# One scratch for q and k, and a ring of packed rows by batch instead of by unit

## What is computed

```python
q = proj(w_q, b_q)          # (16, 16 heads, 256, 8)
k = proj(w_k, b_k)
v = proj(w_v, b_v)
scores = jnp.einsum('bhtd,bhsd->bhts', q, k) / jnp.sqrt(jnp.float32(dk))
attn = jax.nn.softmax(scores, axis=-1)
out = jnp.einsum('bhts,bhsd->bhtd', attn, v)
...
x = x + layernorm(attention(layernorm(x)))
x = x + layernorm(experts(layernorm(x)))
```

## Time and profile before

| | |
|---|---|
| median of 3 runs | 526.82 us (524.11 to 530.07) |
| span of the profiled execution | 525.4 us |
| PE busy | 472.5 us (90%) |
| DVE busy | 404.0 us (77%) |
| ACT busy | 372.3 us (71%) |
| POOL busy | 228.4 us (43%) |
| DMA moved | 67.48 MB, 128 GB/s over the span |

### The profile page before, as it was taken

How to read it: one execution, slowest core, us unless ns; L and a number is a source line. 1 busy time by engine, 2 the same in 40 slices (tenths; PEclk the granted TensorE clock), 3 DMA queues, 4 the chain that set the end, 5 groups by cost and what they waited for, 6 DMA issues and landing times.

```text
span 525.4 us, 11035 instructions
## 1 busy us (share of the span) xinstructions
PE 472.5 (90%) x3416; PEld 276.7 (53%) x3416; DVE 404.0 (77%) x1063; ACT 372.3 (71%) x739; POOL 228.4 (43%) x544
## 2 busy tenths in 40 slices
PE   2458998998999999888899899999999999999994
PEld 1212454544544455444346576666666666666662
DVE  4688898989999999768926859788687959687453
ACT  2315887878989988767684576886868696867551
POOL 6054333325444635221003453938567483716241
PEclk9999999999999999989899999999999999999998
DMA  6443334444444433330023353535444644535431
GB/s 197 134 137 109 118 111 133 127 135 132 122 143 142 134 115 105 119 116 29 3 88 120 118 168 97 189 109 178 141 145 161 179 168 122 194 105 192 133 128 40
DMA packets 51737, 67.48 MB, mean 128 GB/s; under 512 B 4192, under 2 KB 35168, under 8 KB 51680
## 3 DMA queue, kind: packets, MB, share of 16 engines
q1 hardware_dynamic: 51680, 66.78, 41.1%
HBM read 51.17 MB, written 15.20 MB: 126 GB/s over the span
## 4 chain that ended last, share of the span: by engine, by line
PE 59%; SPq 12%; DVE 9%; issue 8%; ACT 5%; DMA 5%; POOL 1%; POOLq 0%; DVEq 0%; ACTq 0%
PE pY L1385 8%; PE pS L1385 8%; SPq L408 6%; PE pS L1369 6%; PE pS L1370 6%; PE pS L1371 6%; PE pO L1304 5%; PE pS L1248 5%; SPq L396 4%; DVE mneg L923 4%; DMA k_scratch<-k_parts 2%; DMA qp<-mT 2%; ACT probs L703 2%; PE pS L1254 2%; SPq L416 2%
## 5 line engine op out<-in xcount | busy, mean ns | idle before, releaser
L923 DVE TENSOR_REDUCE mneg<-pS 128x2 f32<-128x512 f32 x256 | 163.7, 684 | 25.0 <-PE pS L1248 24.5
L703 ACT ACTIVATE probs<-pS 128x512 f32<-128x512 f32 x256 | 144.0, 595 | 29.8 <-PE pS L1254 28.2
L1248 PE MATMUL pS<-kp,qp 48*128 48x256 bf16 x512 | 87.4, 290 | 24.4 <-DVE mneg L923 9.3
L789 ACT ACTIVATE h_ring<-r 128x512 f32<-128x512 f32 x104 | 65.0, 625 | 35.0 <-DVE r L1092 26.2
L1369 PE MATMUL pS<-qp,up_hi 128*128 128x512 f32 x144 | 89.3, 620 | 0.0
L1254 PE MATMUL pS<-qp,kp 51*128 51x256 bf16 x512 | 87.1, 281 | 0.9 <-ACT probs L703 0.7
L1304 PE MATMUL pO<-probs,vv 128*32 128x256 f32 x1024 | 74.5, 398 | 0.4 <-ACT oT_sb L655 0.4
L1248 PEld LDWEIGHTS pS<-kp,qp 48*128 48x128 bf16 x512 | 34.2, 96 | 74.8 <-DVE mneg L923 42.4
L1092 DVE SCALAR_TENSOR_TENSOR r<-pS,probs 128x512 f32<-128x512 f32 x64 | 43.4, 686 | 22.2 <-PE pS L1371 21.7
L1092 DVE SCALAR_TENSOR_TENSOR r<-pS,c_ring 128x512 f32<-128x512 f32 x64 | 44.0, 687 | 17.8 <-PE pS L1371 15.4
L1370 PE MATMUL pS<-kp,up_hi 128*128 128x512 f32 x144 | 57.1, 396 | 0.0
(11 more groups left out here) (193 smaller groups left out, 855.5 us busy)
## 6 DMA issues: line engine op xcount, KB each, us to landing
c_ring<-c_scratch SPq DMA_DIRECT2D x32, 512.0 KB, 4.0
probs<-c_scratch SPq DMA_DIRECT2D x32, 512.0 KB, 4.2
qp<-q_scratch SPq DMA_DIRECT2D x64, 96.0 KB
kp<-k_scratch SPq DMA_DIRECT2D x64, 96.0 KB
q_scratch<-q_parts SPq DMA_DIRECT2D x16, 192.0 KB, 2.4
k_scratch<-k_parts SPq DMA_DIRECT2D x16, 192.0 KB, 2.6
q_scratch<-q_parts SPq DMA_DIRECT2D x16, 128.0 KB, 2.6
k_scratch<-k_parts SPq DMA_DIRECT2D x16, 128.0 KB, 2.3
```

The lines of the kernel that those rows point to most:

```text
L703: nc.scalar.activation(probs[j][:, hh], pS2[n % S2_RING][:, :, :], ACT.Exp, scale=SCALE).then_inc(exp_done, 1)
L789: nc.scalar.activation(h_ring[:, (n - at) % HRING], r_sb[n % URING][:, :], ACT.Square).then_inc(sq_done, 1)
L923: nc.vector.tensor_reduce(mneg[u % 2][:, :, hh, k], pS1[n % S1_RING][:, :].rearrange("p (a s) -> p a s", a=TH), AX.X, ALU.max, negate=True ...
L1248: return mm(pS1[n % S1_RING][:, T * th:T * (th + 1)], qp[slot][rows, k, P * th:P * (th + 1)], kp[slot][rows, k, :], start=True, stop=True)
```

## The change

`q_scratch` and `k_scratch` become one `qk_scratch`, in which q and k of the same feature and position lie side by side. The host permutes the rows of the projection weights so that the features come in the order (half of the block pair, feature, unit, block): the eight blocks of a batch are contiguous for one head half and feature. So the row of one slot and feature holds both units, all four blocks of each, q and k: 8 x 2 x 256 bf16 = 8 KB. `load_batch(b)` fetches 48 such rows per half `hh`, two transfers of 384 KB for a batch, where `load_unit` had four of 96 KB for a unit. The ring has three slots of a batch (BRING = 3) with the same memory as six of a unit. The scratch writes keep their number and sizes; their rows of 512 B go to every second 512 B.

`load_batch(b)` waits for the batch's scratch writes, and from batch 3 on for all key scores of the batch that had the slot. In SP's loop `load_batch(b+2)` stands at the head of iteration b, where `load_unit(2b+5)` stood; `load_unit(2b+6)` falls away there. Ahead of the loop it takes the places of `load_unit(0)` to `load_unit(3)`; unit 4 comes with `load_batch(2)` in iteration 0. TensorE waits for `packed` only ahead of even units.

```diff
+BRING = RING // 2
...
-        q_scratch = nc.dram_tensor("q_scratch", (NB, SLOTS, 4, DK, UB, T), BF16).ap()
-        k_scratch = nc.dram_tensor("k_scratch", (NB, SLOTS, 4, DK, UB, T), BF16).ap()
+        qk_scratch = nc.dram_tensor("qk_scratch", (NB, SLOTS, P, 2, T), BF16).ap()
...
-        qp = [sb(f"qp{i}", [P, UB, T], BF16) for i in range(RING)]
-        kp = [sb(f"kp{i}", [P, UB, T], BF16) for i in range(RING)]
+        qk = [sb(f"qk{i}", [P, 2, UB, 2, T], BF16) for i in range(BRING)]
+        qp, kp = ([qk[i // 2][:, i % 2, :, w] for i in range(RING)] for w in range(2))
...
-                        dst = scratch[b, s:s + n].rearrange("s u d j t -> (u d j) s t")
+                        dst = qk_scratch[b, s:s + n, :, i].rearrange("s p t -> p s t")
...
-            def load_unit(u):
-
-                b, half = divmod(u, 2)
+            def load_batch(b):
+
                 sp.wait_ge(scratch_done[b % 2], N_PARTS * (b // 2 + 1))
-                if u >= RING:
-                    sp.wait_ge(s2_done, TH * UB * (u - RING + 1))
+                if b >= BRING:
+                    sp.wait_ge(s2_done, TH * NBLK * (b - BRING + 1))
                 for hh in range(2):
                     rows = slice(HALF * hh, HALF * hh + QK_ROWS)
-                    for dst, scratch in ((qp[u % RING][rows], q_scratch), (kp[u % RING][rows], k_scratch)):
-                        sp.dma_start(dst, scratch[b, :, 2 * half + hh].rearrange("s d j t -> s d (j t)")
-                                     ).then_inc(packed[u % RING], 16)
+                    src = qk_scratch[b, :, HALF * hh:HALF * (hh + 1)].rearrange("s (d j) w t -> s d (j w t)", d=DK)
+                    sp.dma_start(qk[b % BRING][rows], src).then_inc(packed[b % BRING], 16)
...
             write_parts(0)
             sp.wait_ge(ones_set, 1)
-            load_unit(0)
-            load_unit(1)
+            load_batch(0)
             write_parts(1)
-            load_unit(2)
-            load_unit(3)
+            load_batch(1)
             write_parts(2)
             load_max(0)
-            load_unit(4)
             load_max(1)
...
             for b in range(NB):
-                if 2 * b + 5 < NU:
-                    load_unit(2 * b + 5)
+                if b + 2 < NB:
+                    load_batch(b + 2)
                 if b + 3 < NB:
                     write_parts(b + 3)
                 if 2 * b + 2 < NU:
                     load_max(2 * b + 2)
-                if 2 * b + 6 < NU:
-                    load_unit(2 * b + 6)
                 if 2 * b + 3 < NU:
                     load_max(2 * b + 3)
...
-                ins = nc.gpsimd.memset(kp[i][:, :, :].rearrange("p a b -> p (a b)").bitcast(F32), ONE_TWICE)
+                ins = nc.gpsimd.memset(kp[i].bitcast(F32), ONE_TWICE)
...
-                if k == 0 and hh == 0:
-                    pe.wait_ge(packed[u % RING], 4 * 16 * (u // RING + 1))
+                if k == 0 and hh == 0 and u % 2 == 0:
+                    pe.wait_ge(packed[u // 2 % BRING], 2 * 16 * (u // RING + 1))
...
-        (0, 2, 3, 1) + tuple(range(4, 3 + w.ndim))).reshape(w.shape)
+        (2, 3, 0, 1) + tuple(range(4, 3 + w.ndim))).reshape(w.shape)
```

More of the change, by code:

```diff
@@ L179, in block_kernel @@
         xT = sb("xT", [P, TILE])
-        x_hi, x_lo = ([ring[XSLOT + i][:, :, :].rearrange("p a b -> p (a b)").bitcast(F32R) for i in range(2)]
-                      for ring in (qp, kp))
+        x_hi, x_lo = ([qk[XSLOT // 2][:, half, UB // 2 * i:UB // 2 * (i + 1)].rearrange("p j a b -> p (j a b)").bitcast(F32R)
+                       for half in range(2)] for i in range(2))
         x_cut = sb("x_cut", [P, TILE])
@@ L252, in block_kernel @@
         scratch_done = [sem(f"scratch_done{i}") for i in range(2)]
-        packed = [sem(f"packed{i}") for i in range(RING)]
+        packed = [sem(f"packed{i}") for i in range(BRING)]
         v_done = sem("v_done")
@@ L381, in write_parts @@
             def write_parts(b):
-                for i, (parts, which, scratch) in enumerate(((q_parts[b % 2], Q_PARTS, q_scratch),
-                                                             (k_parts[b % 2], K_PARTS, k_scratch))):
+                for i, (parts, which) in enumerate(((q_parts[b % 2], Q_PARTS), (k_parts[b % 2], K_PARTS))):
                     sp.wait_ge(part3_done, 2 * b + i + 1)
```

## The result

| | before | after |
|---|---|---|
| median | 528.45 us (4 runs, 524.11 to 530.80) | 615.54 us (4 runs, 613.02 to 618.84) |
| span of the profiled execution | 525.4 us | 611.2 us |
| PE busy | 472.5 us | 497.2 us |

The ratio is 1.170, with an interval of 1.164 to 1.176. The direction was forecast, the size was not: 615.5 lies far above the range of 526 to 554.

The account below looks back on a forecast made before the run. SP's issuing and TensorE were taken as bounds side by side. Loop 6.7, start 1.3 and clock 3 added 11.0 to the 525.4 us span, 536.4; with 1.4 from span to median, 538 us, range 526 to 554.

Parts of the forecast that it names:

- What bounds the kernel: In the attention stage, SP's issuing (14.2 us per batch) and TensorE (about 14.5) are bounds side by side.
- what the change removes: On SP, eight load issues per batch become two, relieving 4.7 us per batch and ending 6.4 us of TensorE waits.
- The move and its loop: Loading at the batch's head closes a loop from copy of maxima to j = 4; period 15.1 or 14.6 us, +6.7 total.
- X: Time from the load's issue on SP to its rows in SBUF: 7.3 us, between 7.0 and 8.4.
- the one for the bytes: Within the load, 786 KB on six DMA engines at 24 GB/s each, 145 GB/s together, take 5.4 us.
- 8 KB is nearer to 4 KB than to 2 KB: Reason for giving the load's 8 KB rows the better rate of 4 KB rows, hence 5.4 us.
- the upper bound: Longest time taken for the load's bytes: 6.55 us at the 120 GB/s of the loads before.
- The clock: TensorE's clock falls to half after stalls in the attention stage: two falls in 13 batches at 1.5 us, +3.
- The start: First scores wait for both units until 25.0, and batch 0's j = 4 for its load until 51.9: 1.3 us in all.
- The load is not hidden: Denies the rival that the load lands before j = 4, leaving only SP's relief: 520.4 us, chance 0.08.
- The clock falls in most batches: Rival for the attention stage: slower load, 16.2 us period and six falls to half clock, about 560 us; chance 0.2.
- Costed at nothing: Scratch writes, maxima queued behind the load, SP's wait in load_batch, POOL's memsets and new operand strides add no time.

Follow-up runs that it names:

- the ring by unit: Joint scratch kept, but ring and order of the kernel before: two 192 KB transfers per unit, a batch ahead; 520.81 us, ratio 0.991 to the kernel before.
- sixteen engines: Changed kernel with each half's 48 scratch rows contiguous and loaded as one dimension, twelve scratch writes per batch instead of six; 563.87 us, ratio 1.073.
- the ring of four: Changed kernel with a fourth batch slot and load_batch(b+3) issued in the middle of batch b; 538.98 us, ratio 1.028.
- The loads alone: Ten kinds of loads issued one at a time behind the changed kernel's end, three rounds; the 6 x 8 load as in the change took 6.89, 6.77, 6.41 us.

## Why the prediction was right and wrong

**What bounds the kernel, and what the change removes: right.** Two issues of the new load cost 1.60 us (taken: 0.78 each), the waits for maxima are gone, SP is idle for most of a batch. The relief alone, measured with the ring by unit (four issues per batch instead of two), is 4.6 us (3.0 to 6.3), where the prediction had 6.4 at most.

**The move and its loop: right.** Copy, L413, L433, load, j = 4, copy is the chain of the kernel after, and the period shrinks with its pieces (20.2 in the changed kernel, 16.7 with sixteen engines). Copy to issue was taken at 2.19 and measured 2.04. The place is the cause: moved alone it costs 76 us, taken back (the ring of four, with its fourth slot) it gives 77.

**X: wrong, 10.9 on average instead of 7.3.** The step that failed is the one for the bytes, 5.4 us; in batch 13 they took about 8.5. It took 24 GB/s per engine from the 387 GB/s of the routing weights, which go to 128 partitions, and gave it to six engines that write 48. The loads alone give 82 GB/s for six engines, 14 each, and no more for six than for four. "8 KB is nearer to 4 KB than to 2 KB" fell too: the pace doesn't depend on the row's length. So two halves take 9.6 us, and 11.5 with the fixed 1.9; in the loop X was 10.9 on average, so part of it overlaps. Even the upper bound, 120 GB/s in the window from 33 to 37, was no bound: it is what all transfers moved together in the middle of a backlog, while X ends when the slowest engine ends (129 GB/s in the middle and 96 over the whole in batch 13). Moved to the new place, those same transfers took 9.84. Price: 3.6 us x 13 batches = 47 us.

The figure of 27 GiB/s per engine from the Trainium skill, page DMA: Bandwidth & Descriptors, which the prediction set beside the sum, is refuted for this transfer by the loads alone, which show 14 GB/s per engine. The port rule of the Trainium skill, page SBUF — State Buffer, cited above, bears on the step that failed, and the prediction didn't weigh it.

**The clock: right in kind, wrong in count and place.** It was put outside the loop as two falls of 1.5 us. It falls in each of batches 1 to 13, and inside the loop: j = 4 to copy is 7.5 on average instead of 5.6, where a kernel whose clock stayed up there has 5.48. Price: 1.9 us x 13 = 25, less the 3 that were counted.

**The start: too small.** TensorE's first scores waited until 28.66 (forecast 25.0, before 24.77) and j = 4 of batch 0 began at 59.09 (forecast 51.9, before 50.63): 8.5 us instead of 1.3. The same X did it, twice over: 10.86 us for the first load and 11.02 for that of batch 2.

**Sum.** 11.0 forecast, + 47 (X) + 25 - 3 (clock) - 2 (copy to issue, 0.15 x 13) + 7 (start) = 85, of 85.8 measured.

**Rivals.** The load is not hidden. *The clock falls in most batches* (0.2) was the mechanism that came true, but its 560 us rested on X = 8.4 and six falls. All rivals shared the same two rows for the bytes, so the range was too narrow on that side: one term that multiplies by 13 was known from rows of another shape only.

**Costed at nothing: mostly right.** Among the waits after there is none of TensorE for maxima, and SP's loads waited for scratch landings only in the start (6.3 us and 1.2 us, once each), and the first load is issued at 17.80 instead of 17.71, so the memsets cost next to nothing. The operand strides show no cost either: the ring by unit has them, and a query score takes 289 ns there, 290 before.

## What to carry over

Before merging transfers, look at what waits for the last byte: a merged load gives up the slack of its first half, and if its issue hangs on work that its landing releases, its length counts in full in every turn. Free the slot earlier or split the load by who needs it first; here the joint scratch pays 0.9% when each unit keeps its own transfer and its batch of slack. Price a load by a row of the same shape (rows, partitions, groups), read to its landing; a mean GB/s over a window tells what moved, not when the last engine ends.

## What the runs showed of the hardware

- Over a fixed part estimated at 1.9 us, a load of 48 rows named as 6 x 8 moved 82 GB/s to 48 partitions, no more than one of 32 rows named as 4 x 8 to 32; as 48 contiguous rows it took 4.2 us instead of 6.4 to 6.9.
- Row length of 2, 4 or 8 KB made no difference to the pace; slots 136 KB apart instead of 128, and reading six rows eight times each, made none either.
- SP's issue took 0.64 to 0.84 us for the 6 x 8 and 4 x 8 loads, 0.30 to 0.34 for 32 or 48 contiguous rows, and 0.51 to 0.57 for 64.
- Maxima queued behind the load's 786 KB, 6 KB each, took 8.4 us from the end of their issue to the wake; in the chain of the kernel before such a transfer took 1.9 to 2.5.
- TensorE's granted clock fell during a stall of 4.62 us and was at its lower level for 6.83 us, 4.77 us of the work that followed among them.
